# A three-layer decoder: norms applied on GpSimd, and two more attention steps whose turned operands go by way of DRAM and VectorE

## The reference

```python
# 1: gated attention, 16 heads, q k s of width 64, v g of width 128
z = cumlogsumexp(s); p = exp(s - z); decay = exp(z[t-1] - z[t])
hk = hk * decay + k p^T ; ok = q hk ; pv = softmax(ok)      # scans over the tokens
hv = hv * decay + p v^T ; o = pv hv
o = o * rsqrt(mean(o^2) + eps) * g_norm_weight * silu(g);   y = o @ Wo
# 2: cross attention with ctx
energy = (Wq ctx + bq)^T (Wk ctx + bk); y = x @ softmax(energy)
# 3: feed-forward with 8-bit activations and ternary weights
h = silu(q8(x) @ Wgate) * (q8(x) @ Wup);  y = q8(hadamard(h)) @ Wdown
# after each layer
(x - mean) / sqrt(var + eps)
```

## Time and profile before

| | |
|---|---|
| median of 3 runs | 1489.14 us (1487.88 to 1489.43) |
| profiled execution, its own time | 1489.89 us |
| its span | 1488.1 us |
| TensorE busy | 1449.3 us, 97% |
| VectorE busy | 1090.8 us, 73% |
| ScalarE busy | 639.2 us, 43% |
| GpSimd busy | 435.8 us, 29% |

### The profile page before, as it was taken

One profiled execution on the slowest core, in us unless ns is written; L12 is line 12 of the kernel. 1 busy time (PEld: TensorE's weight loads), 2 busy tenths in 40 slices (PEclk: granted clock), 3 DMA queues, 4 the chain that ended last, 5 costly groups with the idle time before them and its releaser, 6 DMA issues.

```text
span 1488.1 us, 23933 instructions
## 1 busy us (share of the span) xinstructions
PE 1449.3 (97%) x9206; PEld 1170.7 (79%) x9240; DVE 1090.8 (73%) x2060; ACT 639.2 (43%) x1205; POOL 435.8 (29%) x282
## 2 busy tenths in 40 slices
PE   8999999999999999999999999999999898999998
PEld 6888888888888888888888888878888555666675
DVE  5567766676667777776677687687787786977788
ACT  4333333333323333333434334234343457776775
POOL 0311011211205455435454423221421343333320
PEclk9999999999999999999999999999999999999999
DMA  5545433443524454445655311101211125344552
GB/s 157 176 133 132 119 97 103 124 118 95 152 69 136 118 141 127 132 110 134 171 155 160 112 43 51 51 7 36 79 43 49 73 79 184 114 135 140 158 172 91
DMA packets 213297, 166.53 MB, mean 112 GB/s; under 512 B 89664, under 2 KB 174528, under 8 KB 213184
## 3 DMA queue, kind: packets, MB, share of 16 engines
q1 hardware_dynamic: 191920, 133.27, 30.5%
q10 hardware_dynamic: 21264, 31.73, 7.1%
HBM read 115.02 MB, written 49.94 MB: 111 GB/s over the span
## 4 chain that ended last, share of the span: by engine, by line
PE 86%; DVE 7%; DMA 2%; ACT 2%; POOL 2%; issue 1%; SPq 0%; POOLq 0%; ACTq 0%; DVEq 0%
PE bank L486 17%; PE bank L492 17%; PE bank L489 17%; PE bank L719 7%; PE bank L614 4%; PE bank L734 4%; PE bank L755 3%; PE bank L576 2%; PE bank L549 2%; PE bank L600 2%; DVE AM L1194 1%; PE bank L571 1%; PE bank L557 1%; PE bank L584 1%; DVE OKM L1172 1%
## 5 line engine op out<-in xcount | busy, mean ns | idle before, releaser
L486 PE MATMUL bank<-Wh,X 128*128 128x512 f32 x512 | 205.6, 402 | 0.1
L492 PE MATMUL bank<-Wh,X 128*128 128x512 f32 x512 | 200.0, 391 | 0.0
L489 PE MATMUL bank<-Wl,X 128*128 128x512 f32 x512 | 199.3, 389 | 0.0
L486 PE MATMUL bank<-X,Wh 128*128 128x512 f32 x384 | 156.7, 408 | 6.3 <-ACT Wh L812 6.3
L1491 POOL TENSOR_TENSOR Wl<-RAW,Wh 128x512 fp32r<-128x512 f32 (+1 forms) x65 | 112.1, 1735 | 136.8 <-ACT Wh L812 136.6
L492 PE MATMUL bank<-X,Wl 128*128 128x512 f32 x384 | 151.2, 394 | 0.0
L489 PE MATMUL bank<-X,Wh 128*128 128x512 f32 x384 | 150.6, 392 | 0.0
L1509 POOL TENSOR_TENSOR sm<-sm,half 128x8 f32<-128x8 f32 x32 | 52.7, 1648 | 331.9 <-DVE sm L1201 331.9
L1532 POOL TENSOR_TENSOR LO<-M,HI 128x512 fp32r<-128x512 f32 x64 | 82.7, 1292 | 161.7 <-PE bank L728 131.6
L874 ACT ACTIVATE V<-bank 128x256 f32<-128x256 f32 x128 | 49.0, 383 | 183.0 <-PE bank L492 182.8
L719 PE MATMUL bank<-XT,W 128*128 128x512 bf16 x492 | 119.3, 383 | 1.2 <-issue 0.2
(11 more groups left out here) (219 smaller groups left out, 3282.0 us busy)
## 6 DMA issues: line engine op xcount, KB each, us to landing
z_scratch<-EV SPq DMA_DIRECT2D x64, 256.0 KB, 2.1
Z<-z_scratch SPq DMA_DIRECT2D x16, 1024.0 KB, 5.8
o_scratch<-OG ACTq DMA_DIRECT2D x96, 128.0 KB, 2.4
AM<-o_scratch ACTq DMA_DIRECT2D x24, 512.0 KB, 4.6
RAW<-wgT SPq DMA_DIRECT2D x16, 512.0 KB, 4.6
RAW<-wuT SPq DMA_DIRECT2D x16, 512.0 KB, 4.3
RAW<-wdT SPq DMA_DIRECT2D x16, 512.0 KB, 4.4
RAW<-Wo SPq DMA_DIRECT2D x14, 512.0 KB, 4.4
```

The costliest lines, as they stand in the source:

```text
L486: engine.matmul(o, lh(c), rh(c), start=c == 0, stop=False)
L489: engine.matmul(o, lh(c), rl(c), start=False, stop=False)
L492: last = engine.matmul(o, ll(c), rh(c), start=False, stop=c == n - 1)
```

## The change

Three things are changed.

- `MOVED` is 26: steps 24 and 25 too send K, e and the gated values by way of DRAM, and the order `ALONE` holds up to step 26.
- All three norms are applied by GpSimd (`normalise` and `normal`) with the same tensor_scalar; VectorE keeps moments and variances. VectorE waits for GpSimd's result in `finish`, and ahead of bn_aggr in the third layer for the tile before last.
- In the norm of the first layer the four additions of eps and the four powers of a batch become one of each, over four columns.

The diff:

```diff
--- before.py
+++ after.py
@@ -51,7 +51,7 @@
 
 
 
-MOVED = 24
+MOVED = 26
 
 
 def moved(n):
@@ -1240,14 +1240,11 @@
                 engine.bn_stats(st[:, i, :], Y[:, k, :]).then_inc(S[name + "_moments"], 1)
                 dve.wait_ge(S[name + "_moments"], 2 * k + 1)
                 engine.bn_aggr(mv[:, i, :], st[:, i, :]).then_inc(S[name + "_moments"], 1)
-                dve.wait_ge(S[name + "_moments"], 2 * k + 2)
-                engine.tensor_scalar(rs[:, i:i + 1], mv[:, i, 1:2], EPS, None, ALU.add).then_inc(S[name + "_var"], 1)
-
-            def normalise(name, k, i):
-                y = Y[:, k, :]
-                dve.wait_ge(S[name + "_rstd"], k + 1)
-                engine.tensor_scalar(y, y, mv[:, i, 0:1], rs[:, i:i + 1], ALU.subtract,
-                                     ALU.mult).then_inc(S[name + "_applied"], 1)
+
+            def variances(name, k, i, tiles=1):
+                dve.wait_ge(S[name + "_moments"], 2 * (k + tiles))
+                engine.tensor_scalar(rs[:, i:i + tiles], mv[:, i:i + tiles, 1], EPS, None,
+                                     ALU.add).then_inc(S[name + "_var"], tiles)
 
             def scale_rows(b, rows):
                 for i in rows:
@@ -1263,7 +1260,6 @@
                                      negate=True).then_inc(S["e_max"], 1)
 
             def finish(b, i):
-                normalise("n2", 4 * b + i, i)
                 dve.wait_ge(S["n2_applied"], 4 * b + i + 1)
                 engine.tensor_reduce(ax[:, b, 0, i:i + 1], Y[:, 4 * b + i, :], AX.X, ALU.max,
                                      apply_absolute_value=True).then_inc(S["x_absmax"], 1)
@@ -1280,9 +1276,7 @@
                     dve.wait_ge(S["x_absmax"], 4 * b)
                     for i in range(4):
                         centre("n1", 4 * b + i, i)
-                elif stage == "n1":
-                    for i in range(4):
-                        normalise("n1", 4 * b + i, i)
+                    variances("n1", 4 * b, 0, 4)
                 elif stage == "qk_out":
                     for k in range(2):
                         dve.wait_ge(S["qk_hi"], 2 * b + k + 1)
@@ -1319,6 +1313,7 @@
                     engine.tensor_tensor(y, y, bank("xm", b, i)[:], ALU.add).then_inc(S["xm_add"], 1)
                     dve.wait_ge(S["xm_add"], 4 * b + i + 1)
                     centre("n2", 4 * b + i, i)
+                    variances("n2", 4 * b + i, i)
                 elif stage in ("x_round0", "x_round1"):
                     k = int(stage[7])
                     q = ax[:, b, :, 2 * k:2 * k + 2]
@@ -1370,7 +1365,7 @@
                     dve.wait_ge(S["h2_evac"], n + 1)
                     engine.tensor_reduce(fs[:, i % 2, q:q + 1], H2[:, i % 2, 512 * q:512 * q + 512], AX.X, ALU.max,
                                          apply_absolute_value=True).then_inc(S["h_absmax"], 1)
-                elif stage in ("scale", "clamp", "turn_q_out", "add", "normal"):
+                elif stage in ("scale", "clamp", "turn_q_out", "add"):
                     ffn_tile(stage, n)
 
             def ffn_tile(stage, i):
@@ -1415,6 +1410,7 @@
                         dve.wait_ge(S["ffn_add"], 16 + h)
                         engine.bn_stats(st3[:, h, :], y[:, cols]).then_inc(S["n3_moments"], 1)
                     dve.wait_ge(S["n3_moments"], 32)
+                    dve.wait_ge(S["n3_applied"], i - 1)
                     engine.bn_aggr(mv3[:, k, :], st3[:]).then_inc(S["n3_moments"], 1)
                     dve.wait_ge(S["n3_moments"], 33)
                     engine.tensor_scalar(rs3[:, k:k + 1], mv3[:, k, 1:2], EPS, None, ALU.add).then_inc(S["n3_var"], 1)
@@ -1426,13 +1422,10 @@
                     dve.wait_ge(S["ffn_add"], i + 1)
                     engine.bn_stats(st3[:, k, :], y).then_inc(S["n3_moments"], 1)
                     dve.wait_ge(S["n3_moments"], 2 * i + 1)
+                    dve.wait_ge(S["n3_applied"], i - 1)
                     engine.bn_aggr(mv3[:, k, :], st3[:, k, :]).then_inc(S["n3_moments"], 1)
                     dve.wait_ge(S["n3_moments"], 2 * i + 2)
                     engine.tensor_scalar(rs3[:, k:k + 1], mv3[:, k, 1:2], EPS, None, ALU.add).then_inc(S["n3_var"], 1)
-                elif stage == "normal":
-                    dve.wait_ge(S["n3_rstd"], i + 1)
-                    engine.tensor_scalar(y, y, mv3[:, k, 0:1], rs3[:, k:k + 1], ALU.subtract,
-                                         ALU.mult).then_inc(S["n3_applied"], 1)
 
             def attention(stage, n):
                 if stage in ("q", "k", "s", "vg0", "vg1", "vg2", "vg3"):
@@ -1508,9 +1501,17 @@
                     pool.wait_ge(S["vec_made"], 3)
                     engine.tensor_tensor(smv[:, 4, :], smv[:, 3, :], half[:, 0:8], ALU.pow).then_inc(S["o_rstd"], 1)
 
-            def root(name, k, i):
-                pool.wait_ge(S[name + "_var"], k + 1)
-                engine.tensor_tensor(rs[:, i:i + 1], rs[:, i:i + 1], half[:, 0:1], ALU.pow).then_inc(S[name + "_rstd"], 1)
+            def root(name, k, i, tiles=1):
+
+                pool.wait_ge(S[name + "_var"], k + tiles)
+                engine.tensor_tensor(rs[:, i:i + tiles], rs[:, i:i + tiles], half[:, 0:tiles],
+                                     ALU.pow).then_inc(S[name + "_rstd"], tiles)
+
+            def normalise(name, k, i):
+                y = Y[:, k, :]
+                pool.wait_ge(S[name + "_rstd"], k + 1)
+                engine.tensor_scalar(y, y, mv[:, i, 0:1], rs[:, i:i + 1], ALU.subtract,
+                                     ALU.mult).then_inc(S[name + "_applied"], 1)
 
             def cross(stage, b):
                 if stage == "ctx":
@@ -1518,13 +1519,17 @@
                         pool.wait_ge(S["ctx_hi"], b + 1)
                         engine.tensor_tensor(CHL[b][:, 1], CTX[:], CHL[b][:, 0], ALU.subtract).then_inc(S["ctx_lo_g"], 1)
                 elif stage == "centre":
+                    root("n1", 4 * b, 0, 4)
+                elif stage == "n1":
                     for i in range(4):
-                        root("n1", 4 * b + i, i)
+                        normalise("n1", 4 * b + i, i)
                 elif stage in ("xm0_out", "xm1_out", "xm2_out", "xm3_out"):
                     i = int(stage[2])
                     root("n2", 4 * b + i, i)
+                    normalise("n2", 4 * b + i, i)
 
             def ffn(stage, n):
+                k = n % 2
                 if stage == "low":
                     pool.wait_ge(S["h_hi"], n + 1)
                     pool.wait_ge(S["had1"], n - 1)
@@ -1532,10 +1537,14 @@
                     engine.tensor_tensor(LO[:, n % 2, :], M[n % 3], HI[:, n % 3, :],
                                          ALU.subtract).then_inc(S["h_lo"], 1)
                 elif stage == "add":
-                    k = n % 2
                     pool.wait_ge(S["n3_var"], n + 1)
                     engine.tensor_tensor(rs3[:, k:k + 1], rs3[:, k:k + 1], half[:, 0:1],
                                          ALU.pow).then_inc(S["n3_rstd"], 1)
+                elif stage == "normal":
+                    y = Y[:, n, :]
+                    pool.wait_ge(S["n3_rstd"], n + 1)
+                    engine.tensor_scalar(y, y, mv3[:, k, 0:1], rs3[:, k:k + 1], ALU.subtract,
+                                         ALU.mult).then_inc(S["n3_applied"], 1)
 
             engine.memset(HK[:], 0.0).then_inc(S["vec_made"], 1)
             for stage, n in attention_order():
```

## The result

| | before | after |
|---|---|---|
| median | 1488.88 us (1487.88 to 1489.43, 4 runs) | 1497.76 us (1495.72 to 1499.52, 4 runs) |
| profiled execution | 1489.89, span 1488.1 | 1499.18, span 1497.3 |

The change makes the kernel slower: the ratio is 1.0060, with a 95% interval of 1.0042 to 1.0077. The forecast was 1484.0 us, and its range ended at 1489.5.

A forecast was written before the change was run, and what follows sets the result against it. TensorE, busy 97%, was taken as the bound. The terms -3.2 + 2.6 + 0.6 - 1.2 - 1.7 - 0.85 - 1.6 + 0.1 = -5.25 us gave 1484.0 us, range 1480.5 to 1489.5.

The forecast's parts named there:

- the sign itself: The prediction would be wrong in the main if GpSimd took over 1.5 us for a tile.
- Rival 2: GpSimd's normalisation takes 1.85 us, costing the last tile, fourth batch and step 29: 1489 us; chance 0.10.
- TensorE -3.2: Steps 24 and 25 lose 30 transposes on TensorE, 0.76 and 0.85 us per step: 3.2 us less.
- step 25 +2.6: New TensorE wait for OKM, late on VectorE, in up to three pieces: 2.6 us, between 1.0 and 4.
- step 26 +0.6: y's additions directly ahead of the weights make TensorE wait for a weights' output bank: 0.6 us, between 0 and 1.9.
- rival 1: Step 25's wait brings the low clock, and the clock after step 27 still falls: 1487.3 us; chance 0.17.
- Rival 3: VectorE stands for o_scratch in steps 24 and 25, TensorE loses 5.6 us plus clock falls: 1493 us; chance 0.07.
- Step 27, -1.2 and -1.7: Two normalisations leaving VectorE shorten TensorE's waits by 1.2 us; the clock fall behind them goes, 1.7, two chances in three.
- Step 29 -0.85: Fewer VectorE additions and normalisations shorten TensorE's waits of 1.23 and 0.41 us: 0.85 us less.
- fourth batch -1.6: Four normalisations in a row leave VectorE ahead of L1367, removing TensorE's 1.57 us bank wait: 1.6 us less.
- tail +0.1: Only the very last normalisation is on the path, 0.6 us on GpSimd for VectorE's 0.55: +0.1, 0 to 1.3.
- 0.65 for faster: Chance of measuring below 1486.2 us: most of the forecast's 0.53, all of rival 4's 0.13, a little of rival 1.

The follow-up runs named there:

- Experiment 4: The changed kernel with GpSimd's norms as add and mult on a negated mean, at three settings of MOVED: 1485.16 us (26), 1485.46 (24), 1484.71 (25).
- add_form: The changed kernel with the mean negated on VectorE and GpSimd's normalisations as add and mult instead of subtract and mult: 1485.16 us, ratio 0.9977.
- moved_only: The changed kernel with all normalisations back on VectorE, MOVED still 26: 1488.8 us, ratio 1.0000 to the kernel before.
- n2_back: The changed kernel with the second norm alone (16 tiles) back on VectorE: 1496.69 us, ratio 1.0054 to the kernel before.
- root_only: The changed kernel with MOVED at 24 and all normalisations on VectorE, leaving the merged epsilon addition and first-norm root: 1489.20 us, ratio 1.0002.
- the fast form: GpSimd's normalisation as add and mult on a negated mean, in place of the changed kernel's subtract and mult; with MOVED 26 measured 1485.16 us.
- n3_back: The changed kernel with the third norm alone (16 tiles, last layer) back on VectorE: 1496.53 us, ratio 1.0057 to the kernel before.
- norms_only: The changed kernel with MOVED back at 24, all norms still on GpSimd: 1498.37 us, ratio 1.0065 to the kernel before.
- n1_back: The changed kernel with the first norm alone (16 tiles) back on VectorE: 1492.68 us, ratio 1.0027 to the kernel before.

## Why the prediction was wrong, step by step

**The step that failed is the price of GpSimd's normalisation.** It was taken from the add and mult row, 0.6 us, because "subtract and mult are nearer to the first". They are not: 2.08 us, above even the bound from max and min, as the scalars per partition add 0.15 to 1.92. Nothing in the trace before told the two apart; there were two rows far from each other, and the choice between them went by likeness of names. With the price fell what rested on it: that nothing but the very last tile is on the path. The prediction had named the sign itself, over 1.5 us for a tile. Experiment 4 shows that this was the failure, and nearly the only one: at 0.77 us a tile the same change gives 1485.2, where the forecast at 0.6 us had 1484.0.

**The rival that had it, mis-sized.** Rival 2 (0.10) was this case, at 1489. It priced the last tile (+1.2), the fourth batch (+2.3) and step 29 (+0.85), 4.35 us over the forecast, and a little for what GpSimd holds of VectorE. Between the two forms 12.6 us were measured. What it left out: step 30, where the gated values' power is queued behind the norms (51.03 against 48.76 in add_form, +2.3); in step 29 not only the gain goes, but a stop of 2.8 us comes, since VectorE waits inside its queue (49.78 against 44.53 in add_form, 5.3 us, 1.6 of them the clock); the stop of 1.17 us for W; and the clock behind the stop of the fourth batch. Behind the stops of 2.00 and 1.17 us it stayed at 1.00 in the changed kernel. "Its normalisations wait only for its own power and stand where the transposes of x come 5 us later or more" looked at the reader of Y alone. The transposes of x waited 0.26 us. What was late was the work queued behind the norm on GpSimd, and VectorE's queue behind the row maximum.

**TensorE -3.2, step 25 +2.6, step 26 +0.6.** Together 0.0, and moved_only measured 1.0000 (within 1.3 us either way). Singly: step 23 is shorter by 0.73 us (0.76 foreseen). Step 24 wins 0.30 of 0.76, since 0.33 goes to the wait for Et at its end. VectorE, in the changed kernel:

```profile
869.16 0.56 DVE L1109 STREAM_TRANSPOSE Kt<-Kt 128x384 f32<-128x384 f32 x1
869.66 0.66 DVE L1114 STREAM_TRANSPOSE Et<-Et 128x512 f32<-128x512 f32 x1
870.25 1.17 DVE L1198 TENSOR_REDUCE sm<-OG 128x8 f32<-128x1024 f32 x1
...
880.37 0.69 DVE L1172 TENSOR_TENSOR OKM<-bank,ZT 128x512 f32<-128x512 f32 x1
```

and TensorE:

```profile
870.47 0.91 PE L557 MATMUL bank<-Et,Kt 128*128 128x128 f32 x6 [0.33 <-DVE Et L1114]
...
881.12 0.66 PE L584 MATMUL bank<-C,OKM 128*128 128x128 f32 x4 [1.65 <-DVE OKM L1172]
```

OKM was foreseen at 880.53 and starts at 880.37. That this is so near is chance, as step 22 starts 0.7 us later in this profile (768.81 against 768.10): counted from the states of step 22, OKM was foreseen at 112.4 us and comes at 111.6. The forecast let TensorE come 0.76 us earlier and VectorE not; but VectorE had waited 0.62 us for TensorE ahead of the masks (L1194, at 864.59), and it moves forward with it. So the waits are 0.33 + 1.65 = 1.98 us, in two pieces instead of three, and 0.6 less than foreseen. No clock fell there, so rival 1 is out in this place. Step 26 has a wait of 0.81 us, though for U (L1138) and not for a bank of the weights: a right size with a wrong place. Rival 3 did not come: VectorE's waits for o_scratch are 23.9 us in 21 steps, 2.9 at most, against 23.5, 19 and 2.8.

**Step 27, -1.2 and -1.7.** It is 2.24 us shorter in the changed kernel. The wait of 0.58 us is gone, that for AM is 1.76 instead of 2.08 (1.4 foreseen), and the clock stays at 1.00. But the clock's term was luck. In moved_only, n2_back and root_only, which have the waits of the kernel before (0.56 to 0.58 and 2.08 us), it stays at 1.00 too, and in add_form it falls behind one of 1.82. It was also mis-sized: with these waits and no fall the step takes 49.45 to 49.50 us, 1.0 to 1.1 less than before, and not 1.7. The same stretches in moved_only and in add_form:

```profile
990.00:994.00 4.00, 1.92 (x30) 1.73 (x30) 2.89 (x6) 2.55 (x4) 1.85 (x1) 1.00 0.01 4
994.00:998.20 4.20, 3.86 (x29) 3.38 (x29) 3.96 (x11) 2.07 (x4) 3.14 (x3) 1.00 0.22 62
```

```profile
990.00:994.00 4.00, 2.40 (x44) 2.20 (x40) 2.88 (x6) 2.50 (x4) 1.36 (x1) 1.00 0.01 4
994.00:998.20 4.20, 3.99 (x22) 3.99 (x23) 3.96 (x12) 1.56 (x4) 3.32 (x2) 0.63 0.21 62
```

So the norms gave some 1.2 us here (49.50 to 48.29 without the fall), as foreseen, and the 1.7 should have been a chance and not a term.

**Step 29 -0.85, fourth batch -1.6, tail +0.1.** Wrong in the changed kernel, right in the fast form: step 29 is 44.53 there, 1.1 below the 45.61 before (0.6 of it by the merged additions alone, by root_only's 45.02); the wait of 1.57 us at L646 is gone, and the one at L726 is 0.71. In the tail the last tile is 2.08 instead of 0.55 us:

```profile
1492.10 0.56 POOL L1541 TENSOR_TENSOR rs<-rs,half 128x1 f32<-128x1 f32 x1 [1.67 <-DVE rs L1416]
1492.76 2.08 POOL L1546 TENSOR_SCALAR Y<-Y,mv,rs 128x512 f32<-128x512 f32 x1
```

which is 1.5 us on the path; n3_back, which has VectorE's 0.55 there again, measured 1.2 less.

**The chances.** 0.65 for faster stood on a row chosen by likeness; the price was open between 0.55 and 1.85 us, a factor of three, and the range reached just to where the upper end had been costed, with too few of its knock-on stops.

## What to carry to other kernels

Price an operation that moves to GpSimd in its exact form (which two operations, one or two, constants or scalars per partition): here the same normalisation was 2.08 us or 0.77, and the difference of 1.3 us a tile was worth 12.6 us. When work goes to an idle engine, ask not only who reads its result but what is queued behind it there (a small power, a low half), and whether the engine that gave it away now waits for it in the middle of its own queue. A clock that fell behind one stop of one profile is a chance, not a term of the sum.

## What the runs showed of the hardware

- GpSimd's tensor_scalar on 128x512 floats: add and mult together, in either order, 0.62 us with constants and 0.77 with two scalars per partition; every other pair tried 1.91 to 1.92 with constants, and subtract and mult 2.07 with two scalars per partition; one operation alone 1.49 with a constant (subtract), 1.56 to 1.57 with a scalar per partition, even where it is the same add or mult.
- The time of a normalisation on GpSimd hardly depended on its neighbours in the attention (median 2078 ns, least 2070), and did in the last layer (median 2300, most 3044, mean 2526; in the fast form a mean of 1210 against 802). In return VectorE's small tensor_scalars L1323 and L1328 took 0.61 and 1.15 us beside GpSimd's work in step 29 of the changed kernel, and 0.16 and 0.21 in the kernel before; what this costs over the whole kernel was not measured apart.
- The granted clock fell behind a wait of 1.82 us in one kernel and not behind one of 2.08 in another, at the same place of the program (step 27). It fell behind the wait at L591 (step 29) in the changed kernel (2.83 us) and not in norms_only, n1_back and n3_back (2.85), and behind that of 2.00 us in step 30 in n2_back and not in the changed kernel, norms_only and n3_back. What decides stays open here.
- Executions of one kernel differ by the clock: of the 66 of the kernel before that were timed beside the variants, the 14 with a mean granted clock of 0.998 had a median of 1488.0 us, the 23 with 0.996 one of 1490.0. The profiled execution of the kernel before, 1489.89 us, had 0.996.
